# First attention's transposes regrouped by query rows, and the value product cut into seven pieces

## The reference, cut to what matters

```python
HEADS, DIM_HEAD = 16, 64
qkv = x @ w_qkv                                   # per sequence 512 x 3072
sim = einsum('bhid,bhjd->bhij', q * SCALE, k) - |i - j| * slope[h]
sim = where(j > i, -max, sim)                     # causal
attn = softmax(sim, axis=-1)
out = einsum('bhij,bhjd->bhid', attn, v)          # then heads joined, @ w_out + b_out
```

## Time and profile before

| | |
|---|---|
| median of 3 runs | 2475.11 us (2465.77 to 2478.99) |
| the profiled execution's own time | 2475.11 us |
| its span in the profile | 2473.2 us |
| TensorE (PE) busy | 2349.1 us, 95% |
| VectorE (DVE) busy | 1832.7 us, 74% |
| ScalarE (ACT) busy | 1876.5 us, 76% |
| GpSimd (POOL) busy | 1443.5 us, 58% |
| mean granted TensorE clock | 0.982 of full speed |

### The profile page before, as it was taken

The page is one execution under the profiler, slowest core; times in us unless marked ns, Lnnn a source line. Parts: engine busy times, 40 slices in busy tenths (PEclk is TensorE's granted clock), DMA queues, the critical chain, the costliest instruction groups (busy, mean ns, idle before and its releaser), DMA issues.

```text
span 2473.2 us, 82166 instructions
## 1 busy us (share of the span) xinstructions
PE 2349.1 (95%) x32896; PEld 1136.1 (46%) x32896; DVE 1832.7 (74%) x5637; ACT 1876.5 (76%) x4707; POOL 1443.5 (58%) x1356
## 2 busy tenths in 40 slices
PE   6999999999999999999999999999999999999877
PEld 3554444444544444444444544444444444544322
DVE  5568687787877778687787877778786887877674
ACT  4877877877778787877878777887777877787434
POOL 5975574756648466574756657475574756556201
PEclk9999999999999999999999999999999999999877
DMA  3011020200202020020201102020020201102020
GB/s 100 4 38 23 7 58 3 57 6 20 45 3 62 3 57 8 6 58 3 62 3 29 36 7 57 3 57 7 7 58 3 62 2 40 25 3 57 2 56 5
DMA packets 59946, 70.45 MB, mean 28 GB/s; under 512 B 11056, under 2 KB 55344, under 8 KB 56368
## 3 DMA queue, kind: packets, MB, share of 16 engines
q1 hardware_dynamic: 59568, 65.21, 11.4%
HBM read 35.04 MB, written 29.36 MB: 26 GB/s over the span
## 4 chain that ended last, share of the span: by engine, by line
PE 77%; DVE 16%; ACT 3%; issue 2%; DMA 1%; SPq 0%; POOL 0%; POOLq 0%; DVEq 0%; ACTq 0%
PE pj L1595 18%; PE pj L1691 12%; PE sc L1659 10%; PE pj L1721 10%; PE sc L1676 5%; PE sc L1768 5%; PE pj L1707 5%; DVE mx L1362 5%; PE pj L1615 5%; PE sc L1754 4%; DVE pq L1309 4%; PE pj L1585 3%; ACT pt L1044 1%; DVE y L1330 1%; DVE onrm L1372 1%
## 5 line engine op out<-in xcount | busy, mean ns | idle before, releaser
L845 POOL TENSOR_SCALAR pq<-pq,rsum 128x128 f32<-128x128 f32 (+3 forms) x1024 | 1151.8, 1139 | 772.8 <-DVE rsum L1316 771.2
L1362 DVE TENSOR_REDUCE mx<-sc 128x1 f32<-128x512 f32 x1024 | 644.1, 679 | 247.5 <-PE sc L1768 247.1
L996 ACT ACTIVATE pq<-pq,mx 128x128 f32<-128x128 f32 (+3 forms) x1024 | 569.8, 570 | 25.9 <-DVE mx L1309 25.7
L1044 ACT ACTIVATE pt<-sc 128x512 f32<-128x512 f32 x1024 | 543.9, 607 | 36.0 <-PE sc L1754 34.6
L1309 DVE CUSTOM_DVE_ANT_0 pq<-sc,relkey 128x128 f32<-128x128 f32 (+3 forms) x1024 | 448.5, 484 | 158.7 <-PE sc L1659 156.1
L1014 ACT ACTIVATE pt<-sc 128x512 f32<-128x512 f32 (+1 forms) x768 | 376.6, 535 | 162.3 <-PE sc L1676 159.5
L1659 PE MATMUL sc<-K,Q 64*128 64x128 f32 (+3 forms) x2048 | 362.5, 452 | 15.7 <-DVE mx L1309 9.4
L1691 PE MATMUL pj<-pt,v 128*32 128x512 f32 (+3 forms) x4096 | 303.8, 437 | 8.5 <-DVE y L1330 5.7
L1676 PEld LDWEIGHTS sc<-ident,pq 64*128 64x128 f32 x5120 | 200.1, 138 | 189.8 <-issue 99.7
L1595 PE MATMUL pj<-xnT,wqkv 128*32 128x512 f32 x2048 | 263.1, 606 | 4.0 <-ACT xnT L947 2.0
L1676 PE MATMUL sc<-ident,pq 64*128 64x64 f32 x5120 | 234.6, 227 | 7.4 <-DVE mx L1309 4.0
(11 more groups left out here) (117 smaller groups left out, 2836.7 us busy)
## 6 DMA issues: line engine op xcount, KB each, us to landing
scr_p<-y SPq DMA_DIRECT2D x160, 128.0 KB, 2.4
QS<-scr_p SPq DMA_DIRECT2D x30, 384.0 KB, 5.8
KS<-scr_p SPq DMA_DIRECT2D x30, 384.0 KB, 8.5
x_in<-in_L_attn_x SPq DMA_DIRECT2D x16, 256.0 KB, 2.9
scr_p<-tanh SPq DMA_DIRECT2D x32, 128.0 KB, 2.4
out_x<-xres SPq DMA_DIRECT2D x15, 256.0 KB, 2.3
QS<-nrow SPq DMA_DIRECT2D x180, 4.0 KB
wqkv<-in_L_attn_w_qkv SPq DMA_DIRECT2D x1, 1536.0 KB, 6.5
```

The source lines that it names most:

```text
L845: pool.tensor_scalar(rows, rows, rsum[:, row_slot(i, p), c:c + 1], None, ALU.mult).then_inc(s_scl, 1)
L996: act.activation(rows, rows, ACT.Exp, scale=-1.0, bias=mx0[:, row_slot(i, p), c:c + 1], accum_out=lsum[:, row_slot(i, p), c:c + 1]).then_i ...
L1044: act.activation(pt1[:, 2 * (unit % UNITS) + h, :], sc[tile_bank(i, "st1", 2 * n + h)][:, :], ACT.Exp, scale=float(DS) ** -0.25).then_inc( ...
L1362: dve.reduce_max(mx1[:, g % 2, at:at + 1], sc[tile_bank(i, "mx1", 2 * t + h)][:, :], AXIS.X).then_inc(s_mxd1, 1)
```

## The change

The blocks are named (k, q), key block and query row. A group now holds blocks by rows, and the value product takes pieces (k, q, past), key block k onto the query columns of rows q to past-1.

```diff
-TURNED = (((0, 0), (1, 0)), ((0, 1), (0, 3), (1, 1), (1, 3)), ((0, 2), (1, 2)))
-TURN_OFF = {(j, k): (T * j, 2 * T + T * j, 4 * T + 2 * P * j, 2 * T + T * j + 3 * P)[k] for j in range(2) for k in range(NT)}
-TURN_BASE = (0, 2 * T, 4 * T, 5 * T)
+TURNED = (((0, 0), (0, 1), (0, 2)), ((1, 1), (1, 2), (2, 2)), ((0, 3), (1, 3), (2, 3), (3, 3)))
+TURN_BASE = [2 * P * sum(len(group) for group in TURNED[:g]) for g in range(len(TURNED) + 1)]
+TURN_OFF = {(j, *block): TURN_BASE[g] + P * (len(group) * j + n) for g, group in enumerate(TURNED) for j in range(2) for n, block in enumerate(group)}
+TURN_NEEDS = (6, 6, 8)
+PIECES = ((0, 0, 3), (1, 1, 3), (2, 2, 3), (0, 3, 4), (1, 3, 4), (2, 3, 4), (3, 3, 4))
@@ turn_probs
-                if g == 0:
-                    pe.wait_ge(s_scl, i.upto(L0N, 8 * p + 8))
+                if g != 1:
+                    pe.wait_ge(s_scl, i.upto(L0N, 8 * p + TURN_NEEDS[g]))
-                blocks = [(j, k, q) for j, k in TURNED[g] for q in range(k, NT)]
+                blocks = [(j, k, q) for j in range(2) for k, q in TURNED[g]]
@@ pv0
-                for k in range(NT):
+                for k, q, past in PIECES:
                     for j in range(2):
-                        base = 2 * PT0 * (p % 2) + TURN_OFF[j, k]
+                        base = 2 * PT0 * (p % 2) + TURN_OFF[j, k, q]
                         for left in (DH * j, DH * j + QUARTER):
                             r = slice(left, left + QUARTER)
-                            last = pe.matmul(t[r, P * k:T], v0[:, p % NBUF, k, r], pt[:, base:base + WIDTH[k]],
-                                             start=k == 0, stop=k == NT - 1)
+                            last = pe.matmul(t[r, P * q:P * past], v0[:, p % NBUF, k, r], pt[:, base:base + P * (past - q)],
+                                             start=k == 0, stop=k == past - 1)
```

## The result

The changed kernel takes 2485.32 us, median of 20 runs (2474.09 to 2491.38). The kernel before takes 2474.76 us, median of 20 runs (2465.28 to 2479.5). The ratio is 1.0040, with a 95% interval from 1.0027 to 1.0052: slower by 0.4%, some 10 us, clear of zero and under the half percent that the prediction called no change. The forecast was 2477.

The account below looks back on a forecast made before the run. TensorE's own work was taken to bound the kernel: 2475.1 + 2 (steps) - 1 (old wait) + 1 (new wait) = 2477 us, with a range of 2459 to 2493 us to hold 8 in 10.

Parts of the forecast that it names:

- the half percent that the prediction called no change: Whole kernel: about 12 us either way counted as no change; within 0.5% was given chance 0.68.
- What bounds the kernel: Whole kernel: TensorE's own work sets the time, busy 389.8 of 400 us in the steady part.
- Seven steps: Value product: same columns streamed, 24 more MATMULs and weight loads per pair, 0.005 us per added step, +2 us.
- The accumulating rows: Trace lines 1615, 1707 and 1721: narrow against wide steps differ by -0.003 to +0.002 us per step.
- the rival of the exposed fill: Value product: each added step shows its 0.19 us fill, 73 us in all, 2550 us; chance 0.05.
- the 77 us: Value product: the skill page's some 60 cycles per added MATMUL, 2552 us in all; the prediction held the trace against it.
- are covered there and will be here: Value product: weight loads, one per MATMUL, run at the same rate in line 1615, so they add no time.
- The wait for the scaling: Transposes of group 0: no longer waiting for row 3's scaling gains 0 to 5.4 us, taken as 1 us.
- the new wait: Transposes of group 2: waiting for all 8 scalings, met on arrival, costs 0 to 6.4 us, taken as 1 us.
- Transposes, copies, buffers: 40 transposes, 3208 ns of ScalarE copies per pair and the bank rotation all stay the same: 0 us.
- A: TensorE's small waits, mostly for VectorE's maxima: half of their 40.0 us goes, 2457 us; chance 0.15.
- B: ScalarE's longer copies 4 and 5 make it late with the second layer's banks: 20 us, 2497 us; chance 0.12.

Follow-up runs that it names:

- the steps alone: Kernel before with only the value product cut into the seven steps, its groups, waits and copies kept: 1.0051 to the kernel before, 2487.51 us.
- the old wait: The change, with all 8 scalings waited for at group 0 as before and none at group 2: 1.0028 to the kernel before.
- the sizes alone: Kernel before with whole columns in groups of 12, 12 and 16 transposes, four steps, all scalings waited for at group 0: 0.9995, 2472.42 us.

## Why the prediction was right, and where not

*What bounds the kernel.* Right. TensorE is busy 388.3 of 400 us from 1000 to 1400, 97.1%, as the text said it must be.

*Seven steps.* The term of +2 us was sized rightly for what it described: 1.9 us, 0.005 us per added step. The accumulating rows were the right ones, and the rival of the exposed fill (73 us) is out, as is the 77 us worked out from the Trainium skill's TensorEngine Tiling, section Instruction Overhead: 24 MATMULs more cost 0.015 us. The page gives that overhead with the remark that one column takes as long as 60, and steps of 128 columns lie above that. What failed is the sentence that the added weight loads "are covered there and will be here", and with it "it is the same work". They compared the array's time and left out that the instructions themselves are loaded, which was put at nothing. The runs put this in its place: 1.0051 with the steps alone, 1.0012 when the stack loads are small. The four profiles with seven steps everywhere, full loads and strips (the change twice, the old wait, the steps alone) have 7.1, 5.8, 10.0 and 8.5 us of "issue", against 2.7 before. That is some 5 us more. With 1.9 us this makes 7 of the 10.

*The rest of the 10 us* lies for the most part in the same stretches. The second and the sixteenth sequence begin their first value product at these times, in the profile before and in that of the steps alone, both of them taken of executions at or next to the median of their kernel:

```profile
152.56 2.36 PE L1691 MATMUL pj<-pt,v 128*32 128x512 f32 x32
...
2207.30 2.36 PE L1691 MATMUL pj<-pt,v 128*32 128x512 f32 x32
```

```profile
152.81 2.38 PE L1693 MATMUL pj<-pt,v 128*32 128x384 f32 x56
...
2217.40 2.38 PE L1693 MATMUL pj<-pt,v 128*32 128x384 f32 x56
```

From one to the other it is 2054.7 us before and 2064.6 with seven steps. So 9.9 of the 12.4 us between the two spans (2473.2 and 2485.6) arise here, where the granted clock is 1.00 but for one dip of 3.4 us at half clock. "issue" is 5.8 us of the 9.9. A stall costs more than its entry says: sequences without one take 147.55 us in the seven-step trace, the one with 2.11 us of stall 149.93, the one with 0.80 us 148.73, so 0.3 to 0.4 us more than the entry; what makes this addition is not shown. The dip costs 1.7 at most. With small loads the same distance is 2050.6 us with four steps and 2051.5 with seven. The kernel before thus loses 4.1 us to the full loads, and the seven steps 13.1.

The change's own first profile has 2062.0 us there, 7.3 more than before. Its span is still the same, since it was 1.7 us shorter ahead of this stretch and 5.6 behind it. In every profile most of the time at half clock lies in the last 190 us: from 2320 to 2400 us the granted clock was 0.88 in this one, against 0.82 in the profile before. With the steps alone the two ends together are 2.5 us longer than before. No run here holds the clock fixed, so whether the change has a share in the ends stays open.

*The wait for the scaling, the new wait.* -1 and +1 us were guesses about nothing. The two runs without and with the move differ by 0.0002 (1.0028 and 1.0030, each within 0.0013), so together they are 0 as far as that can tell; no run parts them. The text's "met on arrival" was wrong for the weight loads (18.2 us idle) and right for the matmuls.

*Transposes, copies, buffers.* 0 us as predicted, by the sizes alone (0.9995). Copies of 384 columns took 497 ns for 500 worked out.

*The rivals.* A did not come: 41.1 us of waits for 40.0. B did not: L1756 waits for L1046 8.5 us, as before. Neither had the one new wait (5.7 us for the copies of group 0), and with the sizes alone it cost nothing that shows. ScalarE's wait before `att` fell from 72.6 to 44.6 us, 0.22 a pair, a little more than the text allowed, and still covers the longer copies. Yet the time moved to the slower side, by a mechanism that the prediction did not have. That its ranges hold 2485 is luck in this sense: they were left wide for other reasons, and its 0.5% for "no change" covers a loss of 10 us that twenty runs of each kernel show clearly. Its two signs of being wrong (a steady busy share outside 97 to 98%, busy time moved by more than 10 us) could not catch it either: they stayed at 97.1% and 4.5 us.

The sign could have been had from the trace before. Its waits had three of kind "issue", at 486.2, 782.3 and 1520.2 us, at the same place of the sequence and behind 10 us in which the DMA engines were busy to 0.72 to 0.84, and the prediction did not read them. Instructions were counted in the prediction (24 a pair), but priced in array time alone.

## What to carry to other kernels

In a kernel that TensorE bounds, count instructions per microsecond, not per kernel, where large DMAs run: a product cut finer costs almost nothing in the array (0.6 ns per MATMUL here) and can still run TensorE dry behind a burst of loads. A wait of kind "issue" inside a run of matmuls, once a period and at the end of a full DMA stretch, is the sign. Two tests settle it: small loads, and whether an instruction packet is through just before TensorE goes on. To find a small loss, compare distances between the same two steps in two traces, not whole spans. Relaxing a wait paid nothing here, where only weight loads and hardly a matmul (1.2 us) had stood idle for it.

## What the runs showed of the hardware

- TensorE's instructions come over the DMA engines: 24 more packets of 16 KB for 6144 more instructions.
- Behind a burst of data they come late: of 61 stalls in all profiles, the longest 2.94 us, 60 ended 1.2 to 1.6 us after an instruction packet was through. With small loads there was none.
- The Trainium skill, Runtime: NRT & Kernel Launch, section Instruction fetch mechanics, says that the sequencer fetches its instructions over a DMA queue of its own, in blocks of 256, and that the crossing of a block is mostly hidden. The blocks agree with the trace (65 bytes an instruction, 16 KB a packet). "Mostly hidden" holds with small loads (no stall) and not behind full DMA engines (up to 2.94 us).
- With four column strips, cutting a float32 product into steps of 128 columns costs 0.005 us per step, from four to seven and from seven to ten alike (2.088, 2.103, 2.118 us).
- One float32 product of 128 weight columns by 512 shows 0.05 us more busy time than the same in four strips (1.080 against 1.028 us), though it has a quarter of the instructions.
